# Cross-attention evacuations wide and in pairs, the first layer norm in three parts with its rows normalised on POOL, and the first keys and values between the last output products

## The reference, cut to what matters

```python
x = layernorm(x + attn(x, ...))
x = layernorm(x + xattn(x, ctx_512, ...))
x = layernorm(x + ffn(x, ...))

def xattn(q, latent_kv, Wq, Wkv_expand, Wout):     # 16 heads of 32 columns
    qp = q @ Wq.T
    k, v = split(latent_kv @ Wkv_expand.T, 2)
    scores = einsum('bhqd,bhkd->bhqk', qh, kh) / sqrt(32)
    attn = softmax(where(causal, scores, lowest))
    return einsum('bhqk,bhkd->bqhd', attn, vh).reshape(b, sq, H) @ Wout.T

def layernorm(x):
    return (x - mean(x)) / sqrt(var(x) + 1e-5)
```

## Time and profile before

| | us |
|---|---|
| median of three executions | 933.74 |
| the profiled execution | 930.5 |
| its span | 928.6 |
| PE busy | 853.7 (92%) |
| DVE busy | 564.9 (61%) |
| ACT busy | 501.5 (54%) |
| POOL busy | 218.9 (24%) |

### The profile page before, as it was taken

How to read it: one execution, slowest core, us unless ns; L and a number is a source line. 1 busy time by engine, 2 the same in 40 slices (tenths; PEclk the granted TensorE clock), 3 DMA queues, 4 the chain that set the end, 5 groups by cost and what they waited for, 6 DMA issues and landing times.

```text
span 928.6 us, 13310 instructions
## 1 busy us (share of the span) xinstructions
PE 853.7 (92%) x4332; PEld 720.5 (78%) x4332; DVE 564.9 (61%) x1097; ACT 501.5 (54%) x1329; POOL 218.9 (24%) x231
## 2 busy tenths in 40 slices
PE   7978999999999977698887699999999999999997
PEld 5767888888788766576776478988888988889885
DVE  4644654753753677588887946535565665656456
ACT  5415744653752753788787452524474745648140
POOL 0222330240230243233232000240232332321410
PEclk9979999999999997899999799999999999999999
DMA  8022221311311010042130121353465554644422
GB/s 314 8 82 69 99 48 32 119 40 40 112 46 40 29 37 14 1 143 87 54 124 27 42 69 46 109 209 111 150 193 179 185 184 157 207 167 137 137 56 80
DMA packets 33647, 92.50 MB, mean 100 GB/s; under 512 B 6744, under 2 KB 12664, under 8 KB 32449
## 3 DMA queue, kind: packets, MB, share of 16 engines
q1 hardware_dynamic: 22352, 53.81, 18.0%
q0 software_dynamic: 11248, 38.09, 12.6%
HBM read 63.57 MB, written 20.97 MB: 91 GB/s over the span
## 4 chain that ended last, share of the span: by engine, by line
PE 63%; DVE 13%; issue 12%; ACT 8%; POOL 2%; SPq 1%; DMA 1%; ACTq 0%; POOLq 0%; DVEq 0%
PE ps L1304 51%; ACT Pt L672 3%; PE ps L1319 3%; PE ps L1643 2%; DVE kb_lo L863 2%; ACT kb_hi L609 2%; PE ps L1364 1%; PE ps L1633 1%; PE ps L1447 1%; DVE zx_lo L863 1%; DVE acc L950 1%; DVE negmax L934 1%; ACT zx_hi L609 1%; SPq L432 1%; POOL Pt L486 1%
## 5 line engine op out<-in xcount | busy, mean ns | idle before, releaser
L486 POOL TENSOR_TENSOR Pt<-Pt,rowinv 112x448 f32<-112x448 f32 x64 | 59.7, 933 | 269.1 <-DVE rowinv L941 268.8
L672 ACT ACTIVATE Pt<-ps,negmax 112x112 f32<-112x112 f32 x256 | 86.9, 356 | 21.1 <-DVE negmax L934 20.9
L1304 PE MATMUL ps<-x2T_hi,ws_hi 128*128 128x448 f32 x256 | 95.4, 373 | 0.8 <-DVE x2T_lo L863 0.8
L1304 PE MATMUL ps<-x2T_hi,ws_lo 128*128 128x448 f32 x256 | 93.0, 363 | 0.0
L1304 PE MATMUL ps<-x2T_lo,ws_hi 128*128 128x448 f32 x256 | 92.6, 362 | 0.0
L1304 PE MATMUL ps<-w_hi,h_hi 128*128 128x512 f32 x224 | 89.8, 401 | 0.2 <-DVE acc L1199 0.2
L800 ACT ACTIVATE hf<-ps,b 128x448 f32<-128x448 f32 x64 | 40.5, 633 | 88.1 <-PE ps L1304 87.5
L1304 PE MATMUL ps<-w_hi,h_lo 128*128 128x512 f32 x224 | 87.7, 392 | 0.0
L1304 PE MATMUL ps<-w_lo,h_hi 128*128 128x512 f32 x224 | 87.4, 390 | 0.0
L1199 DVE TENSOR_TENSOR acc<-ps,acc 128x512 f32<-128x512 f32 x56 | 38.5, 688 | 52.5 <-PE ps L1304 52.5
L863 DVE TENSOR_TENSOR h_lo<-hf,h_hi 128x448 fp32r<-128x448 f32 x64 | 39.9, 623 | 49.3 <-ACT h_hi L801 49.2
(11 more groups left out here) (290 smaller groups left out, 2346.3 us busy)
## 6 DMA issues: line engine op xcount, KB each, us to landing
stage<-in_wf SPq DMA_DIRECT2D x32, 513.0 KB, 3.8
rows_in<-zero SPq DMA_DIRECT2D x30, 256.0 KB, 3.1
xs<-rows_in POOLq DMA_DIRECT2D x29, 256.0 KB, 4.2
rows_out<-yb POOLq DMA_DIRECT2D x29, 256.0 KB, 2.5
stage<-in_wa SPq DMA_DIRECT2D x4, 1408.0 KB, 6.1
stage<-in_wb SPq DMA_DIRECT2D x4, 1280.0 KB, 5.6
qr<-ro_hi SPq DMA_DIRECT2D x64, 56.0 KB, 1.9
qr<-ro_lo SPq DMA_DIRECT2D x64, 56.0 KB, 1.9
```

The source lines that it names most:

```text
L486: nc.gpsimd.tensor_tensor(p, p, rowinv[0:S, b % 2, :].unsqueeze(2).broadcast_to([S, GH, S]), ALU.mult).then_inc(norm_done, 1)
L672: last = nc.scalar.activation(Pt[0:S, b % 2, h * S:(h + 1) * S], ps[0:S, b % 2, h * S:(h + 1) * S], ACT.Exp, bias=negmax[0:S, b % 2, h:h + 1],
L1304: ins = mm(dst, w, x, start=start and i == 0, stop=stop and i == len(ops) - 1, skip_group_check=not (start and stop))
```

## The change

- **Z of the cross-attention in pairs.** ACT and DVE evacuate it only after an odd batch, two batches (banks 4 and 5) per instruction: 32 partitions by 224 columns instead of 112, four per engine and pair.
- **Keys wide.** ACT and DVE write K as one instruction of 128 partitions by 448 columns each, into new tiles `kx_hi`, `kx_lo`. SP then spreads them into `kb` with eight transfers per half (`spread_keys`), of 32 partitions by 4 by 112 columns. The scores wait for `kb_ld`, the landing of these. The zeros of `kb` come from two transfers of SP out of a zeroed `kx_hi`; ACT's first write of `kx_hi` waits for them (`kb_zero`).
- **Weights.** POOL writes the high parts too (`stage` times a column of ones) before the low ones, for L and X.
- **Layer norms.** The first has three parts, tiles 0 to 3, 4 to 5 and 6; in both the rows are normalised by POOL.
- **Order.** K 0 and V 0 stand between the output products of the last self-attention group. The context and its split come two steps earlier, and the zero blocks of `rows_in` are issued in the self-attention's loop, from a tensor in DRAM. Tiles are laid out anew so that the early ones don't overlap what is still in use.

```diff
-LN_PARTS = [(0, TT - 2), (TT - 2, TT)]
+LN_PARTS = [[(0, 4), (4, 6), (6, TT)], [(0, TT - 2), (TT - 2, TT)]]
+TURN_BANK = [(0, 1, 2, 3, 4, 5, 3), (0, 1, 2, 3, 0, 1, 2)]
...
-    8: [(LAST, "CX"), (LAST, "L"), (NEXT, "Q", 1, 0), ("W", 4), (LAST, "LN1", 0), (NEXT, "Q", 2, 0),
+    8: [(NEXT, "Q", 1, 0), (LAST, "LN1", 0), ("W", 4), (LAST, "K", 0), (NEXT, "Q", 2, 0),
...
-X_START = [("V", 0), ("K", 0), ("Q", 0), ("U1", 5), ("U1", 6)]
+X_DONE = [("K", 0), ("V", 0)]
+X_START = [("Q", 0), ("U1", 4), ("U1", 5), ("U1", 6)]
...
 # SP
+                for i in range(NZERO):
+                    sp.dma_start(rows_in[i, g - 1, :, :], d["zeros"]).then_inc(zero_st, 16)
+            def spread_keys(g, half):
+                cols = slice(half * HALF, (half + 1) * HALF)
+                bs = slice(HB * half, HB * half + HB)
+                sp.wait_ge(x_free["K"], XJ.count(("K", half), g))
+                for dst, src in ((kb_hi, kx_hi), (kb_lo, kx_lo)):
+                    for h in range(GH):
+                        r = slice(DXH * h, DXH * (h + 1))
+                        sp.dma_start(f32(dst[r, bs, h, :]),
+                                     f32(src[r, cols]).rearrange("p (b s) -> p b s", b=HB))\
+                          .then_inc(kb_ld[half], 16)
...
-            sp.wait_ge(sc_done, B * NG)
+            sp.wait_ge(a_free["B"], NG * GH)
             sp.dma_start(cx[:, :, :], d["ctxT"][:, :, 0:S]).then_inc(cx_ld, 16)
+            sp.wait_ge(kx_zero, 1)
+            for t in (kb_hi, kb_lo):
+                sp.dma_start(f32(t[:, :, :, :]).rearrange("p (a c) h s -> p a (c h s)", a=GH),
+                             f32(kx_hi[:, :]).unsqueeze(1).broadcast_to([P, GH, T])).then_inc(kb_zero, 16)
...
 # POOL
+                nc.gpsimd.tensor_tensor(wx_hi[:, 0:X_O], stage[:, 0:X_O], one[:, :].broadcast_to([P, X_O]),
+                                        ALU.mult).then_inc(xl_hi, 1)
...
-                    for t in (kb_hi, kb_lo):
-                        nc.gpsimd.memset(f32(t[:, :, :, :]), 0.0).then_inc(kb_zero, 1)
+                    nc.gpsimd.memset(f32(kx_hi[:, :]), 0.0).then_inc(kx_zero, 1)
+            def normalise_tiles(i, r):
+                pool.wait_ge(ln_inv, ln_part(i, r) + 1)
+                for t in range(*LN_PARTS[i][r]):
+                    nc.gpsimd.tensor_scalar(acc[:, t, :], acc[:, t, :], mv[:, t, 0:1], rstd[:, t:t + 1],
+                                            ALU.subtract, ALU.mult).then_inc(ln_out, 1)
...
 # ACT
-                        act.wait_ge(kb_zero, 2)
-                        for h in range(GH):
-                            r = slice(DXH * h, DXH * (h + 1))
-                            ins = copy(kb_hi[r, HB * j:HB * j + HB, h, :],
-                                       bank[r, 0:HALF].rearrange("p (b s) -> p b s", b=HB))
+                        act.wait_ge(kb_ld[j], 16 + 128 * g)
+                        act.wait_ge(kb_zero, 32)
+                        ins = copy(kx_hi[:, j * HALF:(j + 1) * HALF], bank[:, 0:HALF])
...
-                elif kind == "Z":
+                elif kind == "Z" and j % 2:
                     act.wait_ge(z_done, m + j + 1)
                     for h in range(GH):
                         r = slice(DXH * h, DXH * (h + 1))
-                        ins = copy(zx_hi[r, j * S:(j + 1) * S], ps[r, 4 + j % 2, h * S:(h + 1) * S])
-                    ins.then_inc(z_hi, 1)
+                        copy(zx_hi[r, (j - 1) * S:(j + 1) * S].rearrange("p (b s) -> p b s", b=2),
+                             ps[r, 4:6, h * S:(h + 1) * S]).then_inc(z_hi, 1)
...
 # PE, scores of the cross-attention
-                    pe.wait_ge(x_free["K"], XJ.count(("K", j // HB), g))
+                    pe.wait_ge(kb_ld[j // HB], 16 + 128 * (g + 1))
```

More of the change, by code:

```diff
@@ L165, with __init__ @@
 X_PRE_POOL = weave(range(4), [("N", 0)])
-X_POOL = weave(range(4, 12), [("N", 0), "fill"], wrap=True, fill={4: [(NEXT, "L")], 5: [("X",)]})
+X_POOL = weave(range(4, 12), [("N", 0), "fill"], wrap=True,
+               fill={4: [(NEXT, "L")], 5: [("X",)], 9: [(LAST, "LN2", 0)], 11: [(LAST, "LN2", 1)]})
 class Jobs:
-    def __init__(self, first, pre, body, kinds):
+    def __init__(self, first, pre, body, kinds, done=()):
         self.pre = [i for i in pre if i[0] in kinds]
         self.body = [i for i in body if group_of(i)[1][0] in kinds]
-        self.last = [i for i in self.body if i[0] != NEXT]
-        own = self.pre + self.last
+        every = self.body + [i[1:] for i in body if i[0] == LAST and i[1] in kinds]
+        self.last = [i for i in (j[1:] if j[0] == LAST else j for j in body) if i in every and i[0] != NEXT]
+        own = list(done) + self.pre + [i for i in self.body if i[0] != NEXT]
         self.per = {k: sum(i[0] == k for i in own) for k in kinds}
+        own += [i for i in self.last if i not in own]
         self.rank = {i: sum(j[0] == i[0] for j in own[:n]) for n, i in enumerate(own)}
@@ L298, in build, with gap @@
         xat = ExitStack()
-        x1T_hi, x1T_lo = pair("x1T", [P, KD, T], xat)
-        kb_hi, kb_lo = pair("kb", [P, B, GH, S], xat)
+        def gap(name, upto):
+            sb(name, [P, upto - sum(held)], at=xat)
+            held.append(upto - sum(held))
+        held = [3 * B * S + 2 * X_SIZE + 2 * B * P + KD * T + 2 * T]
         cx = sb("cx", [P, B, S], at=xat)
@@ L359, in build @@
         w_ld = [sem(f"w_ld{k}") for k in range(KD)]
+        kx_zero, one_set = sem("kx_zero"), sem("one_set")
+        kb_ld = [sem(f"kb_ld{half}") for half in range(2)]
         pack_ld = [sem(f"pack_ld{half}") for half in range(2)]
@@ L495, in _ @@
             pool.sem_inc(rot_lo, 1)
+            nc.gpsimd.memset(one[:, :], 1.0).then_inc(one_set, 1)
+            pool.wait_ge(one_set, 1)
             for i, (lo, hi) in enumerate(A_PIECES):
@@ L1535, in x_ready @@
                     pe.wait_ge(x_free[item[0]], XJ.count(item, 0))
+            turns(pe.Fori, AJ, ATT_PRE, ATT_PE, att_step, att_ready)
+            for kind, j in AJ.last[-2:]:
+                if kind == "W":
+                    pe.wait_ge(a_free["W"], 1 + AJ.count((kind, j), NG - 1))
+                else:
+                    pe.wait_ge(x_free[kind], AJ.count((kind, j), NG - 1))
             turns(pe.Fori, XJ, X_PRE_PE, X_PE, x_step, x_ready)
```

178 lines of the change are left out of this document (99 added, 79 removed).

## The result

| | before | after |
|---|---|---|
| median of 20 runs (lowest to highest) | 934.6 us (931.8 to 938.4) | 937.2 us (933.5 to 943.7) |
| ratio, 95% interval | | 1.0030 (1.0016 to 1.0044) |
| profiled execution, its span | 930.5, 928.6 us | 935.4, 933.4 us |
| busy: PE, DVE, ACT, POOL | 853.7, 564.9, 501.5, 218.9 us | 855.2, 533.5, 474.9, 251.6 us |

The changed kernel is slower by 0.3%. 914.6 us was predicted, 904 to 926 as range: wrong by 22.6 us and in sign. DVE lost 31 us of work, ACT 27, and the time did not fall.

What follows compares the result with a forecast made beforehand. PE, ACT and DVE were taken as near their limit, none at it, each waiting for the next. Gains 12 + 2.4 + 1.2 + 3.5 = 19.1 off 930.5 gave 911.4; plus 3.2 for the median, 914.6 us, range 904 to 926.

Steps and rivals of the forecast that it cites:

- The stall and its cause: First layer norm: DVE's five-column step takes 6.68 us because POOL's memsets of kb hold the port; without them about 0.2.
- The other wait: Second layer norm: DVE's weight subtraction beside POOL's tiles 5 and 6 would wait up to 1.8 us, covered by logits' products.
- A tile of 512 columns with one input ... I take 0.9: Layer norms: assumed time in us for POOL to normalise one tile, chosen between 0.56 (memset) and 1.2 (scaled two-input form).
- this term: Last cross-attention group and second layer norm: 3.5 us gained, bounds 1 and 5.
- The passage: Way into the cross-attention through the first layer norm: zeros land at 348.5, first scores at 361, 12 us gained.
- The first four steps: Scores 0 to scores 4 of the first cross-attention group: 2.4 us gained of 16.5, bounds 0 and 4.
- The loops: Cross-attention loop, three times: 34.5 us per group, 0.4 gained in each, 1.2 in all; bounds of a group 31.4 and 36.5.
- my base: Cross-attention loop before the change: period of 34.87 us per group, from which the gain per group was counted.
- the landings take the place of small copies: Cross-attention loop: waits for spread keys' landings replace the small copies' time, leaving only 0.4 us gained per group.
- the second rival: Passage gains without the rest: zeros land at 354 or loops run at 36.5 us per group; 926 us, chance 0.2.
- Slower by spreading: Rival: key spreading on SP and transfer engines costs 3.3 us more per half, landing 4.7 already cancels gain; 938 us, chance 0.05.
- Feed-forward: 0: Feed-forward part, left alone by the change: forecast difference of 0 us.

Runs made afterwards that it cites:

- the two kernels on it: Kernel before with the five-column step as two-input TENSOR_TENSOR: 932.8 us in one run; kernel before with POOL's two memsets cut into sixteen: ratio 1.0008.

## Why the prediction was wrong

- **The stall and its cause: right.** 6.68 us became 0.62, up to the end of POOL's split, and 0.17 where POOL is idle; the two kernels on it showed the mechanism on both sides. The other wait that the prediction took from the same rule didn't come: DVE's weight subtraction, which reads two tiles, started in the midst of POOL's tile 5 and took 1.22 us, as it does alone.
- **"A tile of 512 columns with one input ... I take 0.9": this failed, and decided the sign.** It is 2.07 us, outside the bounds of 0.56 to 1.2. The bounds were from a memset, which reads nothing, and from a two-input form, taken to be dearer than any one-input form; it is the cheaper one. In the second norm 3.5 us of gain were forecast and 8.6 of loss came; with DVE normalising, the stage takes 40.7 us against 41.3 before, so the gain wasn't there either. These 12.1 us are half of the 23.9 between the forecast (-19.1) and the profiles (+4.8). With the norms on DVE the change is faster than the kernel before (0.9933), but by a third of what was forecast. The two bounds of this term, 1 and 5, were both gains: a price that the trace didn't show had been let in with one sign. The Trainium skill, "GPSIMD Engine Reference", section "Engine selection", which I weighed, has one-input work on this engine near line rate; this form isn't (2.07 us, against 0.47 on DVE).
- **The passage: right in kind, 2.9 us short.** The zeros landed at 350.7, inside the bounds (344 to 354). 3584 KB took 15.6 us from the first issue, where I had scaled from the load of the weights to 13.2. (The prediction's 3670 KB are thousands of bytes, and its 1408 KB are of 1024; in one unit its estimate is 0.3 us lower.) From the landing to scores 0 the prediction counted 13.2 us (348.5 to 361.7), and it was 13.2, in part by luck: tile 6 came out of POOL at 363.3, where 359.0 was forecast, and PE waited 0.4 us for it just ahead of scores 0. So 2.2 of the 2.9 are the landing, and 0.7 the step from the sum's 361.7 to 361.
- **The first four steps**: -0.7 instead of -2.4. Variants with this piece unchanged show 15.8 to 18.1 us for it, so it can't be read finer than that.
- **The loops: +3.2 instead of -1.2.** The sum of a group was 34.5; it is 37.0. The pieces were 8.1, 10.2, 8.7 and 9.7 in the first group where 8.0, 9.2, 7.9 and 9.4 were forecast; the chain was right, each link somewhat short. The rest is my base: 34.87 was one group, and the mean of three was 35.9. That the landings take the place of small copies was said at no gain; it cost 1.7 us per group. This is the second rival's 36.5, and a little more, and the period is over the 36 that the prediction named as a sign of being wrong.
- **The last rivals.** "Slower by spreading" named 938 and came to the right time for a wrong reason: landings took 2.1 us, not the 4.7 it needed. The sign came from a mechanism with no rival of its own.
- **Feed-forward: 0 was right** for the change; the 2.8 us of this profile are the stall that went with the set.

## What to carry to other kernels

Before work goes to another engine, bound its price there from rows of the same form of instruction, or leave the range open on the side of loss, above all where its result is waited for. A wait that is removed by a transfer brings the transfer's landing in its place: ask what is queued on each engine that waits for it, and take the zeros from a place that nobody else wants. Undo the parts one at a time: of this change one part cost 8 us, another gave as much, and only the sum was near nothing.

## What the runs showed of the hardware

- POOL's TENSOR_SCALAR over 128 x 512 fp32 with scalars per partition takes 1.56 us with one operation and 2.07 with two; its TENSOR_TENSOR of the same columns 1.04 with one column repeated as the second input and 1.28 with two tiles; DVE's TENSOR_SCALAR with two 0.47.
- DVE's TENSOR_SCALAR of five columns waited while POOL ran a TENSOR_TENSOR and memsets without a gap, over sixteen memsets as over two. Its TENSOR_TENSOR of two inputs waited for POOL's subtraction (to within 0.03 us) and not for the memset behind it; RECIPROCAL passed beside the memset. The Trainium skill, "SBUF — State Buffer", section "Who interferes with whom", has it so: a VectorE instruction with two inputs contends with a GpSimd instruction that reads, not with one that only writes, and the two-port form blocks fully. For POOL's TENSOR_TENSOR and MEMSET these runs agree, and add that the TENSOR_SCALAR isn't let in between instructions that follow without a gap. (A TENSOR_TENSOR was, once: `kvN_lo` ended at 41.06 us, 0.15 after one subtraction of POOL and 2.2 before the end of the next.) For POOL's TENSOR_SCALAR they don't agree: it reads a tile too, and DVE's subtraction of two tiles ran beside it from 533.40 at its usual length (1.22 at 512.28, with POOL idle), in this trace and in five others.

```profile
532.64 4.13 POOL L594 TENSOR_SCALAR acc<-acc,mv,rstd 128x512 f32<-128x512 f32 x2 [4.42 <-DVE rstd L1027]
533.40 1.22 DVE L920 TENSOR_TENSOR ws_lo<-stage,ws_hi 128x1024 fp32r<-128x1024 f32 x1
```

- Two transfers of 1792 KB from SBUF to SBUF, with a source read four times over, landed 8.1 and 14.8 us after their issues: 3584 KB in 15.6 us.
